# VectorE sums a tile's products directly behind making them, and the routing follows three slots nearer

## The reference

```python
# attention, 16 heads of width 8, on the normalised x
scores = jnp.einsum('bhld,bhsd->bhls', Q, K)
out = jnp.einsum('bhls,bhsd->bhld', scores * causal, V)      # no softmax
x = x + (out @ wo_w.T + wo_b)
# experts, on the normalised new x: 8 experts, the best 2 of each token
probs = softmax(xm @ Wg); topk_p, topk_i = top_k(probs, 2)
ye = relu(xs @ W1[e] + b1[e]) @ W2[e] + b2[e]
x = x + scatter_add(ye * p)
```

## Time and profile before

| | |
|---|---|
| median of 3 runs | 280.29 us (279.5 to 280.4) |
| the profiled execution | 280.46 us, span 278.7 us |
| granted TensorE clock, mean | 0.916 of full speed |
| busy, share of the span | PE 82%, DVE 73%, POOL 65%, ACT 61% |
| tile phase | to about 161 us |
| expert phase | from about 158 us to the end |

### The profile page before, as it was taken

One profiled execution on the slowest core, in us unless ns is written; L12 is line 12 of the kernel. 1 busy time (PEld: TensorE's weight loads), 2 busy tenths in 40 slices (PEclk: granted clock), 3 DMA queues, 4 the chain that ended last, 5 costly groups with the idle time before them and its releaser, 6 DMA issues.

```text
span 278.7 us, 6426 instructions
## 1 busy us (share of the span) xinstructions
PE 227.6 (82%) x1418; PEld 175.7 (63%) x1418; DVE 202.1 (73%) x598; ACT 170.7 (61%) x675; POOL 182.0 (65%) x175
## 2 busy tenths in 40 slices
PE   6699889999999999998856279988919999999100
PEld 6354546666666666665545169877909999999000
DVE  5879999889989898999984848844502555554852
ACT  3543358888989898878697146655604767766000
POOL 3329961123868878687737777777777777777750
PEclk9999999999999999999995559999965999999855
DMA  6980000000100101011101272233445333438984
GB/s 203 280 246 0 2 1 0 2 0 12 41 30 30 41 30 42 29 38 39 51 29 48 67 166 69 59 105 103 115 131 142 107 98 88 125 101 294 330 228 136
DMA packets 32425, 25.49 MB, mean 91 GB/s; under 512 B 4334, under 2 KB 30192, under 8 KB 32390
## 3 DMA queue, kind: packets, MB, share of 16 engines
q1 hardware_dynamic: 23824, 14.52, 19.4%
q0 software_dynamic: 4320, 8.47, 9.1%
q10 hardware_dynamic: 4246, 2.10, 2.6%
HBM read 13.92 MB, written 11.61 MB: 92 GB/s over the span
## 4 chain that ended last, share of the span: by engine, by line
PE 55%; DVE 17%; DMA 10%; issue 8%; POOL 3%; ACT 3%; SPq 2%; POOLq 1%; DVEq 1%; ACTq 0%
PE ps L971 16%; PE ps L1063 8%; PE ps L1074 7%; PE ps L939 6%; DMA returned<-y_sb,xt 4%; POOL returned L417 3%; DVE back L680 3%; PE ps L980 2%; DMA xt<-dispatched 2%; PE ps L1056 2%; PE ps L991 2%; PE ps L962 2%; DVE back L671 2%; DVE o_sb L693 2%; PE ps L983 1%
## 5 line engine op out<-in xcount | busy, mean ns | idle before, releaser
L389 POOL DMA_INDIRECT dispatched<-rows,slot x64 | 65.8, 1028 | 37.5 <-ACT rows L482 17.0
L417 POOL DMA_INDIRECT returned<-y_sb,xt x71 | 71.1, 1002 | 21.6 <-issue 17.1
L971 PE MATMUL ps<-back,causal 128*128 128x512 f32 x128 | 61.9, 606 | 0.0
L881 DVE TENSOR_SCALAR y_sb<-ps,xt 128x128 f32<-128x128 f32 x71 | 24.9, 350 | 47.1 <-PE ps L1075 46.8
L1063 PE MATMUL ps<-xT,w_of 128*128 128x128 f32 x284 | 49.9, 301 | 1.2 <-DVE w_of L876 0.7
L1074 PE MATMUL ps<-w_sb,hT 128*128 x284 | 45.7, 285 | 0.1
L564 ACT ACTIVATE hT<-ps,b_col 128x128 f32<-128x128 f32 x142 | 44.2, 367 | 1.2 <-PE ps L1063 0.7
L373 POOL TENSOR_TENSOR back<-qkv 128x1024 f32<-128x1024 f32 x16 | 31.3, 1954 | 20.8 <-ACT qkv L503 20.6
L556 ACT ACTIVATE xT<-ps 128x128 f32<-128x128 f32 x71 | 19.7, 278 | 38.2 <-PE ps L1056 37.0
L1063 PEld LDWEIGHTS ps<-xT,w_of 128*128 128x128 f32 x284 | 39.8, 203 | 3.3 <-ACT xT L556 2.0
L680 DVE TENSOR_TENSOR back<-ps,qkv 128x1024 f32<-128x1024 f32 x32 | 38.9, 1216 | 2.1 <-PE ps L971 2.0
(11 more groups left out here) (171 smaller groups left out, 422.2 us busy)
## 6 DMA issues: line engine op xcount, KB each, us to landing
xt<-dispatched SPq DMA_DIRECT2D x71, 65.0 KB, 1.9
back<-returned SPq DMA_DIRECT2D x7, 512.0 KB, 6.4
x_sb<-x SPq DMA_DIRECT2D x8, 256.0 KB, 5.3
out<-x_sb ACTq DMA_DIRECT2D x7, 256.0 KB, 3.6
returned<-y_sb,xt POOLq DMA_INDIRECT x71, 2.5
w_sb<-w SPq DMA_DIRECT2D x1, 1024.0 KB, 5.7
w_sb<-w SPq DMA_DIRECT2D x2, 512.0 KB, 7.6
dispatched<-rows,slot POOLq DMA_INDIRECT x64, 2.3
```

Of the source, the lines that this page charges most:

```text
L389: pool.indirect_dma_start(out=dispatched[:, :], out_offset=bass.IndirectOffsetOnAxis(ap=slot[:, g * K + k:g * K + k + 1], axis=0), in_=row ...
L417: pool.indirect_dma_start(out=returned[:, :], out_offset=bass.IndirectOffsetOnAxis(ap=xt[:, n % G, D:D + 1].bitcast(I32), axis=0), in_=y_s ...
L971: mm = pe.matmul(ps_run[g % 2][:, u, :], causal[:, :], outer[:, g % OUTER_RING, 512 * u:512 * (u + 1)], start=True, stop=True)
```

## The change

On DVE `attend_sum(g)` moves from slot g+1 to slot g, directly behind `attend(g)`. `state_out` moves from lag 2 to 1, `add_residual` from 5 to 3, `softmax_start` from 8 to 5, `softmax_end` and `places` from 9 to 6. On PE `q_transposed` goes from 5 to 3, `o_transposed` and `project_out` from 7 to 5, `sum_state` from 5 to 4, `transpose2` from 10 to 7, `gate` from 11 to 8, `rank` from 12 to 9. On ACT the whole routing row goes from 10 to 7, with the stages behind it. POOL's `dispatch` goes from slot g+16 to g+13. The tails get shorter by what the loops now reach, the waits that guard shared PSUM banks get new numbers, and the counts of the first five batches are now read inside the loops: PE issues `count_first` in slot 33 in front of `sum_state(29)` and waits there for `cnt_read`; DVE makes that copy in its slot 30, behind `attend_sum(30)`.

```diff
-    STATE_AFTER = 7
+    STATE_AFTER = 5
@@ POOL
-            for s in range(N + 16):
-                if s >= 16:
-                    dispatch(s - 16)
+            for s in range(N + 13):
+                if s >= 13:
+                    dispatch(s - 13)
@@ ACT
-            tile_stages = [(10, mean2_out), (12, exponentials), (10, spread2_out), (0, qkv_out), (10, variance_log2), (11, xn2T_out), (10, scale2_out),
-                           (-1, xnT_out), (10, shift2_out), (6, qT_out), (10, rows_out), (-2, normalize), (7, oT_out), (13, chosen),
+            tile_stages = [(7, mean2_out), (9, exponentials), (7, spread2_out), (0, qkv_out), (7, variance_log2), (8, xn2T_out), (7, scale2_out),
+                           (-1, xnT_out), (7, shift2_out), (4, qT_out), (7, rows_out), (-2, normalize), (5, oT_out), (10, chosen),
...
-            exponentials(N - 2 * T - 1)
-            xn2T_out(N - 8)
-            qT_out(N - 3)
-            oT_out(N - 4)
-            qT_out(N - 2)
-            row_of(N - 7)
+            xn2T_out(N - 5)
             qT_out(N - 1)
-            oT_out(N - 3)
-            chosen(N - 2 * T - 1)
-            row_of(N - 6)
             oT_out(N - 2)
-            row_of(N - 5)
             oT_out(N - 1)
...
+            exponentials(N - T - 1)
             last_deviation()
-            exponentials(N - T - 1)
@@ DVE
-            tile_stages = [(5, add_residual), (9, softmax_end), (1, attend_sum), (8, softmax_start), (0, attend), (0, scales_ahead),
-                           (9, places), (2, state_out), (-2, outer_product), (-2, statistics_ahead)]
+            tile_stages = [(3, add_residual), (6, softmax_end), (5, softmax_start), (0, attend), (0, attend_sum), (0, scales_ahead),
+                           (6, places), (1, state_out), (-2, outer_product), (-2, statistics_ahead)]
             for s in range(-2, N):
                 for lag, stage in tile_stages:
+                    if s == N - 2 and stage is state_out:
+                        count_first()
...
-            count_first()
-            state_out(N - 2)
-            add_residual(N - 5)
-            softmax_end(N - 2 * T - 1)
-            attend_sum(N - 1)
+            last_statistics(N - 4)
+            add_residual(N - 3)
+            last_statistics(N - 3)
             state_out(N - 1)
-            places(N - 2 * T - 1)
-            for g in range(N - T, N):
+            softmax_start(N - T - 1)
+            for g in range(N - 2, N):
                 add_residual(g)
                 last_statistics(g)
             last_shift()
-            softmax_start(N - T - 1)
@@ PE
-            tile_stages = [(3, running_sums), (11, gate), (5, q_transposed), (7, o_transposed), (5, sum_state), (-1, project),
-                           (-2, transpose1), (10, transpose2), (7, project_out), (12, rank)]
+            tile_stages = [(3, running_sums), (8, gate), (3, q_transposed), (5, o_transposed), (4, sum_state), (-1, project),
+                           (-2, transpose1), (7, transpose2), (5, project_out), (9, rank)]
             for s in range(-2, N + 3):
                 for lag, stage in tile_stages:
-                    if s == N + 2 and stage is sum_state:
+                    if s == N + 1 and stage is sum_state:
                         count_first()
+                        pe.wait_ge(cnt_read, 1)
...
+            sum_state(N - 1)
+            gate(N - 5)
             last_o_transposed(N - 2)
-            rank(N - 2 * T - 1)
             last_project_out(N - 2)
-            last_transpose2(N - 6)
             last_o_transposed(N - 1)
             last_project_out(N - 1)
-            last_transpose2(N - 5)
-            last_gate(N - 7)
-            last_gate(N - 6)
-            last_gate(N - 5)
             last_transpose2(N - 4)
```

More of the change, by code:

```diff
@@ L193, in preln_linear_attention_moe @@
         ps_cnts = ps[0:1, 1, D + E:D + E + QE]
-        ps_qT_last = [ps[:, 0, 0:P], ps[:, 0, P:2 * P]]
-        ps_att_last = [ps[:, 7, 0:P], ps[:, 5, 0:P], ps[:, 4, 0:P], ps[:, 5, 0:P]]
+        ps_att_last = [ps[:, 4, 0:P], ps[:, 5, 0:P]]
         ps_T2_last = [ps[:, 2, 0:P], ps[:, 3, 0:P]]
@@ L532, in qT_out @@
                 wait(act, oT_mm, g + 1 - T)
-                act.activation(qT[:, g % T, :], ps_qT if g < N - 2 else ps_qT_last[g + 2 - N], ACT.Identity).then_inc(qT_done, 1)
+                act.activation(qT[:, g % T, :], ps_qT, ACT.Identity).then_inc(qT_done, 1)
             def oT_out(g):
@@ L542, in xn2T_out @@
                 wait(act, lg_mm, g + 1 - RING)
-                act.activation(xn2T[:, g % RING, :], ps_T2 if g < N - 7 else ps_T2_last[g % 2], ACT.Identity).then_inc(xn2T_done, 1)
+                act.activation(xn2T[:, g % RING, :], ps_T2 if g < N - T else ps_T2_last[g % 2], ACT.Identity).then_inc(xn2T_done, 1)
             bias_at = {}
@@ L661, in add_residual @@
                 wait(dve, att_mm, g + 1)
-                dve.tensor_tensor(tile(g), ps_att if g < N - T else ps_att_last[g + T - N], tile(g), ALU.add).then_inc(x2_done, 1)
+                dve.tensor_tensor(tile(g), ps_att if g < N - 2 else ps_att_last[g + 2 - N], tile(g), ALU.add).then_inc(x2_done, 1)
             def outer_product(g):
@@ L927, in transpose1 @@
                 wait(pe, xnT_done, g)
-                wait(pe, oT_done, g - 8)
+                wait(pe, oT_done, g - 6)
                 pe.transpose(ps_T1, xn[:, g % RING, :], ident[:, :]).then_inc(T1_done, 1)
@@ L935, in project @@
                 wait(pe, qkv_done, g)
-                wait(pe, shift_done, batches(g - 12))
+                wait(pe, shift_done, batches(g - 9))
                 if g == 0:
@@ L948, in q_transposed @@
                 wait(pe, qkv_done, g + 1)
-                wait(pe, xnT_done, g + 7, N)
+                wait(pe, xnT_done, g + 5, N)
                 wait(pe, qT_done, states(g) - 1)
-                wait(pe, xn2T_done, g - 5)
+                wait(pe, xn2T_done, g - 4)
                 pe.transpose(ps_qT, qkv[:, g % QKV_RING, 0:D], ident[:, :]).then_inc(qT_mm, 1)
@@ L978, in o_transposed @@
                 wait(pe, qT_done, states(min(g + 1, N - 1)))
-                wait(pe, xn2T_done, g - 3)
+                wait(pe, xn2T_done, g - 2)
                 mm = pe.matmul(ps_oT, o_sb[:, g % RING, :], ident[:, :], start=True, stop=(g % T == 0))
@@ L995, in transpose2 @@
                 wait(pe, rows_done, g + 1)
-                wait(pe, oT_done, g + 4, N)
+                wait(pe, oT_done, g + 3, N)
                 wait(pe, xn2T_done, g)
@@ L1001, in gate @@
                 wait(pe, xn2T_done, g + 1)
-                wait(pe, qkv_done, g + 12, N)
+                wait(pe, qkv_done, g + 9, N)
                 wait(pe, shift_done, batches(g - 1))
@@ L1015, in rank @@
                 wait(pe, before_done, b + 1)
-                wait(pe, x2_done, g + 5, N - T + 1)
+                wait(pe, x2_done, g + 4, N - 2)
                 wait(pe, placeof_done, b)
@@ L1098, in last_o_transposed @@
                 wait(pe, oT_done, g)
-                wait(pe, qT_done, states(N - 3))
-                wait(pe, xn2T_done, N - 7)
+                wait(pe, qT_done, states(N - 1))
+                wait(pe, xn2T_done, N - T)
                 mm = pe.matmul(ps_oT, o_sb[:, g % RING, :], ident[:, :], start=True, stop=(g % T == 0))
                 if g % T:
-                    wait(pe, qT_done, states(g))
                     wait(pe, state_done, states(g))
@@ L1109, in last_project_out @@
                 wait(pe, oT_done, g + 1)
[L1110 to L1115, removed]
-                att = ps_att_last[g + T - N]
+                wait(pe, prod_done, N)
+                att = ps_att_last[g + 2 - N]
                 pe.matmul(att, oT[:, g % RING, :], wo_sb[:, :], start=True, stop=False)
@@ L1122, in last_transpose2 @@
                 wait(pe, prod_done, N - 1)
-                if g >= N - 5:
-                    wait(pe, xn2T_done, g - 1)
+                wait(pe, xn2T_done, g - 1)
                 pe.transpose(ps_T2_last[g % 2], rows[:, g, 0, 0:D], ident[:, :]).then_inc(T2_done, 1)
@@ L1128, in last_gate @@
                 wait(pe, xn2T_done, g + 1)
[L1129 to L1146 removed]
+                wait(pe, state_done, states(N - 1))
+                pe.matmul(ps_lg_last[:, g % T, :], xn2T[:, g % RING, :], wg_sb[:, :], start=True, stop=True).then_inc(lg_mm, 1)
+            sum_state(N - 1)
+            gate(N - 5)
             last_o_transposed(N - 2)
[L1148 removed]
             last_project_out(N - 2)
[L1150 removed]
             last_o_transposed(N - 1)
             last_project_out(N - 1)
[L1153 to L1156 removed]
             last_transpose2(N - 4)
```

34 lines of the change are left out of this document (removed).

## The result

| | before | after |
|---|---|---|
| median, run in turn on one chip | 280.35 us | 292.34 us |
| lowest and highest of the four | 279.5 to 283.74 us | 290.7 to 292.58 us |
| the profiled execution | 280.46 us, span 278.7 | 290.7 us, span 288.9 |
| granted TensorE clock, mean | 0.916 | 0.93 |

The changed kernel is slower: ratio 1.0407, 95% interval 1.0343 to 1.0471. The forecast was 279.8 us with a range to 283.2; the result lies 9 us above the range. Two further executions of the changed kernel, outside this median, took 289.45 and 291.36 us. The profiled execution is the shortest of the four: it is 10.2 us longer than the one before, while the medians lie 12.0 apart. What follows explains the 10.2.

A forecast was written before the change was run, and what follows sets the result against it. POOL's queue from 144.55 was taken to set the end, PE mostly the tile phase. Terms summed to -0.1 us for batch 6's places, POOL's lost backlog gave -0.5; 280.46 - 0.6 = 279.9, forecast 279.8 us, range 276.8 to 283.2.

The forecast's parts named there:

- Steady stretch +0.2: Five steady rounds of four tiles: VectorE still fits at 15.5 against 15.98 us; +0.2 us, bounds -1.0 to +2.5.
- Rival B: Steady rounds: VectorE's and POOL's outer products block each other over SBUF; 283 to 285 us, in full 287; chance 0.15.
- Warm-up +1.0: Start to the end of slot 9: extra PE work and a wait for the first state_out; +1.0 us, bounds 0.2 and 2.3.
- Count read +2.3: Round's end: PE stands still about 4.1 us for the counts' copy, costing VectorE 2.3 us; bounds 1.5 and 3.
- clock +2.3: Behind PE's wait for the counts: TensorE's clock falls to 0.50, costing 2.3 us.
- A (the clock stays): Rival: the clock stays at full after the count wait, so 2.3 drops out; 277.5 us, chance 0.20.
- C (the wait is short): Rival: PE's count wait is 2 us, not 4, the clock holds, VectorE loses 1.5; 276.5 us, chance 0.10.
- D's small waits: Rival: warm-up and small PE waits add up to the upper bounds, +3; 282.5 us, chance 0.10.
- Tail -3.0, -2.1, -0.5: Savings: attend(31) to attend_sum(31) 3.0 us, from there to project_out(31) 2.1, from there to batch 6's places 0.5.
- `pick` wait: Sign in the steady rounds: VectorE's 0.63 us wait at `pick` goes to near 0.
- POOL's run from batch 6 on has no gap: Sign at the end: POOL works gaplessly from the places of batch 6, near 153.6, no longer from 144.55.

The follow-up runs named there:

- e1: The changed kernel, with one wait more: POOL's products of an even tile wait for VectorE's of the odd tile in front; 282.48 us, ratio 1.0114.
- e3: The changed kernel with POOL's dispatches put back to slot g+16; 284.66 us, ratio 1.021.
- e4: e1 with VectorE copying the counts one slot earlier, in slot 29 in front of outer_product(31); 278.96 us, ratio 0.9961.
- e8: e4 with attend_sum moved behind places and state_out in the same slot; 275.63 us, ratio 0.9852.
- e9: e4 with attend_sum put back to slot g+1, as in the kernel before, first in the tail; 276.99 us, ratio 0.9895.
- e11: e8 with ScalarE's chosen one slot later, after qT_out (lag 11 for 10); 329.33 us on other chips, ratio 1.0215 to the kernel before.
- e13: The kernel of e11 run once more; 333.39 us on other chips, ratio 1.0284 to the kernel before.
- e2: The kernel before with only attend_sum(g) moved directly behind attend(g), all other lags as before; 293.46 us, ratio 1.0534.
- e5: The changed kernel with only the counts copied one slot earlier, the products still overlapping; 287.1 us, ratio 1.0254.

## Why the prediction was wrong, point by point

**The step that failed is "Steady stretch +0.2", with its bound of +2.5 for the five rounds.** They took 9.5 us more: 89.12 from 47.86 to 136.98, against 79.63 before (57.05 to 136.68). Of that 8.1 are the meetings. The overlap of the two products had been left out of this term. Rival B named the mechanism, the place (POOL's product at 6.9 to 8.9 behind a round's start, VectorE's at 7.8) and a full price of 287, and got a chance of 0.15. Two things were wrong in how it was set aside.

First, the meeting was treated as a chance one. It is fixed. Both engines start from the same event in each round, `softmax_end` on VectorE: it releases `chosen` on ScalarE, that releases POOL's four dispatches (93.48 on, 1.26 each), and behind them POOL's product begins at 98.29, while VectorE's own list brings it to its product at 98.05. In the kernel before only two dispatches stood in between. When VectorE is held up, the next `softmax_end` is late by the same amount, and the pair meets again. Delay doesn't move them apart: the five meetings cost alike.

Second, the price was added up too low. Per round it was right: 17.75 - 16.21 = 1.54 where 1.9 - 0.4 = 1.5 was forecast. Four of these and a first one of 1.9 make 8.1. The meeting in the warm-up, which the prediction's steps did not look for, adds 1.3 (the running sums that start at 40.44 in e1 start at 41.73). That is the 9.4 that e1 gives back. With five times 1.5 B came to 287; the rest up to 292.3 is mainly this meeting and the 2.7 us by which e1's median, free of meetings, lies above the forecast.

In the Trainium skill, "SBUF — State Buffer", section "SBUF: two separate sides", a VectorE instruction with two SBUF inputs and a GpSimd instruction that reads SBUF exclude each other by a lock that is held for a whole instruction, and the one that starts first has it. By that rule, the trace agrees on the first half, 3.30 us for a 1.22 us instruction. On the second half the records give VectorE's as the earlier (98.05 against 98.29) and yet POOL's ran first, at its full speed. So the recorded starts don't tell who goes first. In all five steady meetings one of POOL's dispatches was still running when VectorE's record begins (97.32 to 98.27 here) and POOL's product begins directly behind it; yet beside such a dispatch alone VectorE's product is not held up (e1: 1.22 from 77.16, dispatch 76.53 to 77.48). What decides the order stays open.

**Round without the meetings: +0.23 each, where +0.2 was forecast for all five.** It is 16.21 in e1, e3, e4, e8 and e9. Over the five rounds e1 is 1.4 us longer than the kernel before (80.99 against 79.63), as the last one is 16.13 for 15.70. The forecast put its 0.11 a tile on the dependent pair; e8 and e9 show that the pair isn't the reason, e11 and e13, for the first full round, that `chosen` is.

**Warm-up +1.0: right, but for the meeting.** The first full slot's running sums start at 40.44 in e1, forecast 40.5, before 39.5. PE's wait for the first state_out ends at 27.15 after 1.30, forecast 1.5 at 27.5.

**Count read +2.3 and clock +2.3: right in mechanism, the clock's too large.** PE's wait was 4.07 for 4.1, and the clock fell to 0.50 behind it. The last running sums took 3.63 for 1.94, 1.7 more, where the 2.3 had 1.77 for them and 0.6 for their neighbours. Rivals A (the clock stays) and C (the wait is short) fall by that; of D's small waits the runs showed 1.4 us, those of the rounds. Taken away in e4, the two give 3.8 at the last `attend` and 3.1 at POOL, not 4.6; the last `attend` less the clock's 1.7 leaves 2.1 for the read.

**Tail -3.0, -2.1, -0.5: about right.** attend_sum(31) stands 1.25 behind attend(31), as forecast. From there to the last projection e1 needs 4.47 for 4.15, and from there to the places of batch 6 5.28 for the 5.74 forecast (6.24 before). The slips in the prediction's own arithmetic change nothing: 280.46 - 0.6 - 0.17 is 279.7 and not 279.8, and the forecast plus D's 3 is 282.8 and not 282.5.

**The `pick` wait vanished and POOL's run from batch 6 on has no gap**, as forecast. With the meetings out, e1's POOL begins batch 6 at 155.82 for the forecast 154.3: the rounds' 1.4 for 0.2 is most of that. Its profiled execution took 280.71 us for the 279.9 forecast, but it was the shortest of ten.

## What to carry to other kernels

Where two engines can hold each other up without a semaphore, write down for each such pair of instructions when both run in the new order, counted from the event that releases both. If the two delays are nearly equal, the meeting comes back in every round and is the likeliest case, not a rival. A wait that fixes the order was worth 9.4 us here; POOL, the engine that then waits, had idle time to spare.

Moving work nearer is worth what the tail gains only if the read that used to stand behind the last large matmul doesn't come in front of it: one slot earlier for the counts gave 3.1 us, and the state copy in front of the sum nearly 2 more. The best version measured (e8) is 1.5% faster than the kernel before. What pays seems to be the nearer routing and the shorter tail: e9, with the sum back in the next slot, is 1.1% faster.

## What the runs showed of the hardware

- A VectorE product of two SBUF operands took 3.30 to 3.64 us (3.69 in e2) in the steady stretch where it meets POOL's, and 1.22 alone; POOL's took 1.96 in both cases. A partial meeting costs as much of the wait as is left: 2.02 at 112.85 in e2, with POOL's from 111.81 to 113.77.
- It isn't always VectorE that gives way. In the warm-up of e2 VectorE's product took 1.30 and POOL's, recorded 0.19 later, 2.92 (e5: 1.58 and 2.92):

```profile
22.25 1.30 DVE L671 TENSOR_TENSOR back<-qkv 128x1024 f32<-128x1024 f32 x1
...
22.44 2.92 POOL L373 TENSOR_TENSOR back<-qkv 128x1024 f32<-128x1024 f32 x1
```

- POOL's indirect DMA behind such a meeting took 1.81 us for 0.96 alone, while VectorE did its product. VectorE lost nothing by it (3.30 is 2.21 of waiting and 1.09 of work). In the kernel before the dispatch at 116.26 took 1.68, beside VectorE's product at 115.89. Both end 0.8 to 0.9 us behind VectorE's product (102.23 against 101.35, 117.94 against 117.11), and so do those of e1, e2 and e3; in e1 and e3 a dispatch that had begun before the product kept its 0.96.
- Half clock: four running-sum passes took 3.63 us in the changed kernel and 1.94 at full clock, after PE had stood still for 4.07 us. The granted clock was still 1.00 in the windows of that standstill (145 to 149) and fell only when PE worked again, in the window from 149 on. In e1, after the same 4.07 us, it fell at the end of the standstill (0.67 from 139 to 140), and the four passes took 2.90.
